# Taking the row maxima off two attention score slots in one pass of four 32-row matmuls

## What is computed

```python
q = l2norm(q) * q_scale
k = l2norm(k) * k_scale
sim = jnp.einsum('bhid,bhjd->bhij', q, k) * SCALE
sim = jnp.where(full_mask, sim, max_neg)
attn = jax.nn.softmax(sim.astype(jnp.float32), axis=-1)
out = jnp.einsum('bhij,bhjd->bhid', attn, v)
return layer_norm(out @ Wo, ln_o_w, ln_o_b)
```

## Time and profile before

| | before |
|---|---|
| median of 3 runs | 801.37 us (801.15 to 801.73) |
| the profiled execution: time, span | 803.27 us, 801.5 us |
| PE busy | 786.7 us, 98% of the span |
| DVE busy | 482.4 us, 60% |
| ACT busy | 321.4 us, 40% |
| POOL busy | 332.1 us, 41% |

### The profile page before, as it was taken

One profiled execution on the slowest core, in us unless ns is written; L12 is line 12 of the kernel. 1 busy time (PEld: TensorE's weight loads), 2 busy tenths in 40 slices (PEclk: granted clock), 3 DMA queues, 4 the chain that ended last, 5 costly groups with the idle time before them and its releaser, 6 DMA issues.

```text
span 801.5 us, 12996 instructions
## 1 busy us (share of the span) xinstructions
PE 786.7 (98%) x4358; PEld 483.7 (60%) x4359; DVE 482.4 (60%) x902; ACT 321.4 (40%) x499; POOL 332.1 (41%) x252
## 2 busy tenths in 40 slices
PE   8999999999999999999999989999999999999997
PEld 4444455554555545555554556656558999999554
DVE  3887777677786878686876855547123333333154
ACT  3455545555655556556554321121112333333110
POOL 2200045758586785858586133203560000000364
PEclk9999999999999999999999999999999999999999
DMA  3014800010001010000020112880522222222244
GB/s 119 27 36 152 262 23 1 1 28 1 28 1 29 0 29 2 20 9 2 27 66 28 27 30 76 267 267 38 184 96 62 93 92 92 92 92 79 79 131 125
DMA packets 53125, 56.39 MB, mean 70 GB/s; under 512 B 9290, under 2 KB 47700, under 8 KB 53076
## 3 DMA queue, kind: packets, MB, share of 16 engines
q1 hardware_dynamic: 49844, 47.23, 18.9%
q0 software_dynamic: 3072, 8.39, 3.2%
q10 hardware_dynamic: 160, 0.14, 0.0%
HBM read 36.73 MB, written 18.67 MB: 69 GB/s over the span
## 4 chain that ended last, share of the span: by engine, by line
PE 87%; issue 5%; POOL 3%; DVE 2%; DMA 1%; ACT 1%; POOLq 1%; DVEq 0%; SPq 0%; ACTq 0%
PE bank L1023 14%; PE score_banks L996 13%; PE score_banks L1248 11%; PE score_banks L1183 8%; PE score_banks L868 7%; PE bank L957 6%; PE bank L1257 5%; PE bank L1198 5%; PE score_banks L1001 4%; PE bank L868 4%; PE bank L941 2%; POOL slot_result L830 2%; PE bank L1183 2%; PE bank L1089 1%; PE score_banks L1238 1%
## 5 line engine op out<-in xcount | busy, mean ns | idle before, releaser
L1595 DVE TENSOR_REDUCE mx<-bank 128x1 f32<-128x512 f32 x248 | 159.3, 685 | 43.7 <-PE bank L957 42.6
L1371 ACT ACTIVATE prob<-score_banks,zero 128x1024 f32<-128x1024 f32 x128 | 142.6, 1116 | 85.3 <-PE score_banks L1001 78.7
L750 POOL TENSOR_TENSOR acc<-acc,prob 128x1024 f32<-128x1024 f32 (+1 forms) x67 | 160.6, 2397 | 22.2 <-DVE tail L1622 10.7
L1023 PE MATMUL bank<-prob,vn 128*64 128x512 f32 x512 | 121.1, 602 | 0.0
L830 POOL DMA_INDIRECT slot_result<-slot_results,posi x32 | 30.3, 947 | 163.8 <-DMA slot_results<-yo 148.9
L1183 PE MATMUL score_banks<-xfT,w12s 128*128 128x512 f32 x208 | 93.3, 593 | 0.8 <-ACT xfT L1432 0.8
L1248 PE MATMUL score_banks<-xsT,w_slot 128*128 128x128 f32 x752 | 91.9, 275 | 1.0 <-ACT xsT L1466 1.0
L1248 PEld LDWEIGHTS score_banks<-xsT,w_slot 128*128 128x128 f32 x752 | 89.2, 192 | 6.0 <-ACT xsT L1466 1.6
L742 POOL TENSOR_TENSOR acc<-prob 128x1024 f32<-128x1024 f32 x16 | 38.3, 2395 | 107.5 <-DVE on L1650 50.2
L1023 PEld LDWEIGHTS bank<-prob,vn 128*64 128x64 f32 x512 | 32.2, 136 | 58.2 <-issue 43.9
L1183 PEld LDWEIGHTS score_banks<-xfT,w12s 128*128 128x128 f32 x208 | 39.3, 190 | 40.8 <-issue 39.7
(11 more groups left out here) (200 smaller groups left out, 1126.6 us busy)
## 6 DMA issues: line engine op xcount, KB each, us to landing
w12r<-in_L_ffn_routed_w SPq DMA_DIRECT2D x32, 256.0 KB, 4.0
slot_rows<-zrow SPq DMA_DIRECT2D x47, 128.0 KB, 1.8
xsl<-slot_rows SPq DMA_DIRECT2D x47, 128.0 KB, 2.0
slot_results<-yo SPq DMA_DIRECT2D x47, 128.0 KB, 1.7
w3r<-in_L_ffn_routed_w SPq DMA_DIRECT2D x16, 256.0 KB, 3.1
rec<-row_sum_reciprocals SPq DMA_DIRECT2D x30, 128.0 KB, 2.9
xin<-in_x SPq DMA_DIRECT2D x16, 128.0 KB, 2.0
w12s<-in_L_ffn_shared_w SPq DMA_DIRECT2D x2, 1024.0 KB, 7.7
```

The costliest lines, as they stand in the source:

```text
L750: g.tensor_tensor(acc[rows, c, :, :], acc[rows, c, :, :], prob[rows, n % PROBS, :, :], ALU.add).then_inc(summed, 1)
L1023: last = mm_(o_bank(i, c)[rows, :], vn[:, kt, b, (2 * j + h) * DH:(2 * j + h + 1) * DH], prob[:, n % PROBS, h, :], start=(s == 0), stop=(s ...
L1371: a(prob[rows, held % PROBS, :, :], score_banks[n % 2][rows, :, :], ACT.Exp, bias=bias[rows, :])\
L1595: v.tensor_reduce(mx[:, h, t, c:c + 1], ring_bank(u)[:, :], AX.X, ALU.max).then_inc(ring_used, 1)
```

## The change

`zneg` now holds every head's negated maxima twice, and its transpose puts them on four groups of 32 partitions: group 2k + h has head h, copy k. `own_tile` gets four diagonals in place of two, so `neg_max` carries both heads in partitions 0 to 63 and again in 64 to 127. The new `take_maxima(i, s, k, opens)` adds the maxima of slot s to its two banks with two 32-row matmuls on groups 2k and 2k + 1.

In each phase the first slot's maxima (k = 0, closing its banks) and the second slot's (k = 1, opening its banks ahead of its scores) are issued together: four matmuls of 32 rows into four banks. The second slot then has its three score passes alone, the last of which counts on `scores_made`. The third slot keeps a pass of its own, of two 32-row matmuls. The number of matmuls stays 288; the passes of maxima go from 144 to 96. VectorE's `negate` issues two reductions in place of one, and GpSimd makes two more diagonals once.

```diff
-    zneg = sb("zneg", [P, 2, DH], stack=att)
+    zneg = sb("zneg", [P, 2, 2, NEG_ROWS], stack=att)
...
-        for r in (0, DH):
+        for r in range(0, P, NEG_ROWS):
             g.affine_select(out=own_tile[:, :], in_=own_tile[:, :], compare_op=ALU.not_equal, fill=1.0,
...
+        def take_maxima(i, s, k, opens):
+
+            two = score_banks_of(i, s)
+            queries = score_place(s)[1]
+            for h in range(2):
+                at = slice((2 * k + h) * NEG_ROWS, (2 * k + h + 1) * NEG_ROWS)
+                last = mm_(two[h][:, :], ones_r[at, :], neg_max[at, queries], start=opens, stop=not opens,
+                           skip_group_check=True)
+                if not opens:
+                    last.then_inc(scores_made, 1)
...
-            for lhs, rhs in ((k_hi[p], q_hi[p]), (k_hi[p], q_lo[p]), (k_lo[p], q_hi[p])):
+            for k, (lhs, rhs) in enumerate(((k_hi[p], q_hi[p]), (k_hi[p], q_lo[p]), (k_lo[p], q_hi[p]))):
                 for h, rows in enumerate((LOW, HIGH)):
-                    mm_(two[h][:, :], lhs[rows, keys], rhs[rows, queries], start=(lhs is k_hi[p] and rhs is q_hi[p]),
-                        stop=False)
-            if s in (0, BOTH + 1):
-                pe.wait_ge(ring_used, ring_freed("neg", i, c))
-            for h, rows in enumerate((LOW, HIGH)):
-                mm_(two[h][:, :], ones_r[rows, :], neg_max[rows, queries], start=False, stop=True)                    .then_inc(scores_made, 1)
+                    last = mm_(two[h][:, :], lhs[rows, keys], rhs[rows, queries], start=(k == 0 and not opened),
+                               stop=(k == 2 and opened), skip_group_check=True)
+                    if k == 2 and opened:
+                        last.then_inc(scores_made, 1)
...
-                        score_slot(i, slots[a])
+                        score_slot(i, slots[a], a == 1)
+                        if a == 0 and f in NEG_AT:
+                            pe.wait_ge(ring_used, ring_freed("neg", i, NEG_AT[f]))
+                        if a != 1:
+                            take_maxima(i, slots[a], 0, False)
+                        if a == 0:
+                            take_maxima(i, slots[1], 1, True)
...
-            v.tensor_reduce(zneg[:, :, tiles], mx[:, :, tiles, :], AX.X, ALU.max, negate=True).then_inc(neg_ready, 1)
+            v.tensor_reduce(zneg[:, 0, :, tiles], mx[:, :, tiles, :], AX.X, ALU.max, negate=True)
+            v.tensor_reduce(zneg[:, 1, :, tiles], mx[:, :, tiles, :], AX.X, ALU.max, negate=True).then_inc(neg_ready, 1)
```

More of the change, by code:

```diff
@@ L60 @@
 RING = 3
+NEG_ROWS = P // 4
 BOTH = TQ
@@ L681, in _ @@
             g.memset(buf[:, :], value)
-        g.memset(zneg[:, :, :], 0.0)
+        g.memset(zneg[:, :, :, :], 0.0)
         g.memset(ones_r[:, :].bitcast(F32), 1.0)
@@ L976, in turn_neg, with score_place, score_banks_of, score_slot @@
             pe.wait_ge(neg_ready, 2 * i + z + 1)
-            nc.tensor.transpose(dst[:, 0:P], zneg[:, :, :].rearrange("p a d -> p (a d)"), ident[:, :])\
+            nc.tensor.transpose(dst[:, 0:P], zneg[:, :, :, :].rearrange("p k a d -> p (k a d)"), ident[:, :])\
                 .then_inc(ring_made, 1)
-        def score_slot(i, s):
+        def score_place(s):
+            c, kt = (0, s) if s <= BOTH else (1, TQ if s == BOTH + 1 else s - BOTH - 2)
+            return slice(kt * P, (kt + 1) * P), slice(c * QC, (c + 1) * QC)
+        def score_banks_of(i, s):
+            n = SLOTS * i + s
+            wait(pe, probs_ready, 2 * (n - 1))
+            return bank[2 * (n % 2)], bank[2 * (n % 2) + 1]
+        def take_maxima(i, s, k, opens):
[7 more added lines that the diff above has]
+                    last.then_inc(scores_made, 1)
+        def score_slot(i, s, opened=False):
             p = i % 2
             n = SLOTS * i + s
-            two = bank[2 * (n % 2)], bank[2 * (n % 2) + 1]
-            wait(pe, probs_ready, 2 * (n - 1))
+            two = score_banks_of(i, s)
             if s == 0:
@@ L991, in score_slot @@
                 pe.wait_ge(v_used, late_count(TQ - 2))
-            c, kt = (0, s) if s <= BOTH else (1, TQ if s == BOTH + 1 else s - BOTH - 2)
-            keys, queries = slice(kt * P, (kt + 1) * P), slice(c * QC, (c + 1) * QC)
-            for lhs, rhs in ((k_hi[p], q_hi[p]), (k_hi[p], q_lo[p]), (k_lo[p], q_hi[p])):
+            keys, queries = score_place(s)
+            for k, (lhs, rhs) in enumerate(((k_hi[p], q_hi[p]), (k_hi[p], q_lo[p]), (k_lo[p], q_hi[p]))):
                 for h, rows in enumerate((LOW, HIGH)):
-                    mm_(two[h][:, :], lhs[rows, keys], rhs[rows, queries], start=(lhs is k_hi[p] and rhs is q_hi[p]),
-                        stop=False)
-            if s in (0, BOTH + 1):
-                pe.wait_ge(ring_used, ring_freed("neg", i, c))
-            for h, rows in enumerate((LOW, HIGH)):
-                mm_(two[h][:, :], ones_r[rows, :], neg_max[rows, queries], start=False, stop=True)                    .then_inc(scores_made, 1)
+                    last = mm_(two[h][:, :], lhs[rows, keys], rhs[rows, queries], start=(k == 0 and not opened),
+                               stop=(k == 2 and opened), skip_group_check=True)
+                    if k == 2 and opened:
+                        last.then_inc(scores_made, 1)
         def weigh(i, s):
```

## The result

The changed kernel takes 824.66 us (median of 4 runs, 824.19 to 825.03) where the kernel before, run beside it, takes 801.55 (801.15 to 802.16). The ratio is 1.0276 with a 95% interval from 1.0255 to 1.0296: 23.1 us slower, where 22.7 were forecast. Measured again on another occasion, it was 824.54 to 802.89, ratio 1.0259 (1.0226 to 1.0293).

A forecast was written before the change was run, and what follows sets the result against it. The prediction took TensorE, busy 344.5 of 345.9 us in stage B, as the bound. Shape changes add 20.7 us over seven pairs, plus 1.5 and 0.5 in the last: 801.4 + 22.7 = 824.1 us, range 811 to 831.

The forecast's parts named there:

- The removed pass is worth nothing: Second slot's pass, 0.23 us, 48 times: VectorE's 1.25 us chain stays, so removal gains nothing 45 times, 0.23 three times.
- Each change of shape costs 0.10 into it and 0.10 of uncovered load: Around 32-row passes in stage B: next pass 0.33 us behind instead of 0.23, first pass recorded 0.50 instead of 0.40.
- Four matmuls run as one pass, their loads side by side: Shared pass of first and second slots: one pass of about 0.50 us; bounds otherwise +0.23 a pass, +4.8 us for loads.
- Piece to piece 1.28 with VectorE as releaser: Between the pieces ahead of second and third slots: VectorE's maxima still release the load, 1.28 us instead of 1.25.
- Phase by phase: Additions in a pair's phases 0 to 5: 0.65, some 0.40, 0.47, 0.47, 0.49, 0.47 us; 2.95 us a pair.
- The total: Seven pairs 20.7, last pair's phases 0 to 2 1.5, its phases 3 to 5 0.5: 22.7 us more.
- no drain: Rival: going between 64 and 32 rows costs nothing, shared pass 0.23 us behind scores; 801.4 or 800.7 us; chance 0.08.
- covered loads: Rival: shape changes cost only 0.10 in and 0.10 out, loads hidden; some 10 us more, 812 us; chance 0.08.
- two passes: Rival: the shared pass's four matmuls do not run as one, or load two by two; 829 to 834 us; chance 0.11.

The follow-up runs named there:

- undoing one of the two visits: Changed kernel with the third slot's pass back at two 64-row matmuls; 814.89 us, ratio 1.0159.
- three visits: Changed kernel with nothing shared: each of a phase's three slots has its own pass of two 32-row matmuls; 837.45 us, ratio 1.0429.
- the run where GpSimd is named as releaser: Kernel before with VectorE's maxima over 64 of 512 columns, exponentials halved from the second pair on, second slot's pass left out; 784.55 us, ratio 0.9768.
- the four on the slower chip: Kernel before with maxima halved, with and without second slot's pass: 800.79, 800.11 us; exponentials halved too, with and without it: 799.76, 794.72 us.
- the order without the shapes: Kernel before with the second slot's maxima opening its banks ahead of its scores, as their own pass of two 64-row matmuls; 806.41 us, ratio 1.0051.

## Why the prediction was right

- *The removed pass is worth nothing.* Right, and shown directly: 1.0001 with the pass left out, six unchanged intervals from piece to piece, and a gain that grows only as VectorE's and ScalarE's chains are shortened.
- *Each change of shape costs 0.10 into it and 0.10 of uncovered load.* Right: 0.33 in and 0.42 to 0.43 out in the changed profile; undoing one of the two visits gave back 1.32 of a forecast 1.36 us a pair, and adding one (three visits) cost 1.55 of an expected 1.6.
- *Four matmuls run as one pass, their loads side by side.* Right: 0.50 for all four, the same as for two, and 0.73 when forced onto the same groups.
- *Piece to piece 1.28 with VectorE as releaser.* Right, 322.55 to 323.83.
- *Phase by phase.* Distances from the transposes of `zneg` to the first `weigh`, and from there from `weigh` to `weigh`, give for phases 0 to 5 an addition of 0.66, 0.22, 0.48, 0.52, 0.49 and 0.47 us; forecast were 0.65, 0.40, 0.47, 0.47, 0.49 and 0.47. The one mis-sized term is phase 1. Ahead of it the kernel before had a small wait that I had overlooked, in its timeline of PE.

```profile
285.01 0.59 PE L1023 MATMUL bank<-prob,vn 128*64 128x512 f32 x1
285.70 1.06 PE L1034 MATMUL bank<-acc,ones_r 128*32 128x512 f32 x8
```

From the last `weigh` pass to the row sums are 0.69 us. In the changed kernel the same step takes 0.53, that is 0.43 from pass to pass there and 0.10 for the change of shape:

```profile
295.89 0.60 PE L1042 MATMUL bank<-prob,vn 128*64 128x512 f32 x2
296.42 1.07 PE L1053 MATMUL bank<-acc,ones_r 128*32 128x512 f32 x8
```

The wait was for GpSimd, the same one as above. Its last addition, in the kernel before and in the changed one (timelines of POOL):

```profile
283.20 2.35 POOL L756 TENSOR_TENSOR acc<-acc,tail 128x1024 f32<-128x1024 f32 x1
293.38 2.35 POOL L757 TENSOR_TENSOR acc<-acc,tail 128x1024 f32<-128x1024 f32 x1
```

Before, the row sums start 2.50 us behind it (285.70), exactly as in the run where GpSimd is named as releaser, and they do so, within 0.01, in all seven pairs that have this step. In the changed kernel they start 3.04 behind it (296.42): the 0.66 us that phase 0 loses covered the wait. The forecast had left this wait out. So a pair grew by 2.85 us, not 2.95.

- *The total.* In the two profiled executions the seven distances from pair to pair grew by 20.1 us together, where the forecast had 20.7. The last pair's phases 0 to 2 grew by 1.35 us (1.5 forecast), and TensorE's sequence in its phases 3 to 5 by 0.87 (from the transposes to the last `weigh`, 20.75 to 21.62), where the prediction worked out 1.1 and counted half without a row that says half. That is 22.3 us in stage B, against 22.7. The rest of the measured 23.1 us is no larger than what runs differ by outside stage B: its first transposes stand at 105.80 us before and 104.41 changed, and from the last score pass to the end are 349.22 and 350.24 us, where the other runs, but for the four on the slower chip, have 349.85 to 352.69. So the mechanism and the size of the pair are shown, and that the total came within 0.4 us is in part luck.

The rivals fall with this: no drain (the 0.33), covered loads (the 0.50 pieces), two passes (0.50 for four). The Trainium skill, "TensorEngine Tiling (Array Packing)", section Tiling Modes, Key Properties, says that a change of mode drains TensorE. This case's trace agrees also from 64 to 32 rows, with a next pass 0.33 behind in place of 0.23. The Trainium skill, "TensorE: Matmul & The Clock Gate", section Measured speedup vs the span model, gives 3.07 times for four row tiles of K = 32, N = 512. Here four such matmuls occupied 0.43 us on four groups and 0.66 on two, which agrees that they run side by side; none of the runs has the four one after another, so the factor itself is not measured.

None of the runs with the reference's full work beats the kernel before. The nearest, the order without the shapes, is 0.5% behind it.

## What to carry to other kernels

Packing small matmuls into more row groups saves passes only among neighbours of the same shape. Count the visits, not the matmuls: here a lone pass in another shape occupied 0.43 us against 0.23, with a further 0.10 ahead of it, and a second pass during the same visit only 0.23. Over a pair a visit cost 0.22 us (1.32 us for six, undone) to 0.24 (4.40 for eighteen), about what one pass of 0.23 is worth where nothing else holds TensorE. So a visit must save more than one pass to pay.

Before taking work off a busy engine, look who stands beside it at that very place. PE, busy for 98% of the span, was held there by VectorE and behind it by ScalarE, and at another place of the pair by GpSimd. The sign in the profile was a weight load whose releaser is another engine, while the matmul row shows little or no gap; for GpSimd in the kernel before it was a fixed distance from another engine's instruction.

## What the runs showed of the hardware

- A weight load for row groups that are in use starts with the matmul ahead and is hidden as long as the shape stays (309.70 in the earlier trace rows). After a change of shape it starts with its own matmul, and that matmul is recorded with 0.50 instead of 0.40 us, for two row groups and for four alike.
- A load that a wait holds back does the same (311.51 in the earlier trace rows, recorded with 0.50 in the earlier trace rows), and its releaser is seen on PEld: in the changed kernel the load at 323.83 stood idle 0.52 us, while the matmul ahead is recorded until 323.74 and leaves only 0.09 idle on PE.
